# Local attention: the mask instruction scales by the inverse norm and keeps the minimum of negated logits

## The reference, cut to what matters

```
q, k, v = split(shift_token(x) @ wqkv)            # 8 heads of 64
q = l2norm(q) * q_scale;  k = l2norm(k) * k_scale
q, k = rotary_xpos(q, k)
sim  = einsum(q * 8, k)                           # windows of 64: own window and the one before
sim  = where(mask, -finfo.max, sim)               # i < j, or i > j + 64, or j outside
attn = softmax(sim)
x    = x + (attn @ v) @ wo
```

## Time and profile before

| | |
|---|---|
| median of 3 runs | 1843.05 us (1841.29 to 1848.9) |
| profiled execution, span from the first to the last instruction | 1846.8 us |
| busy in it: TensorE, ScalarE, VectorE, GpSimd | 1709.5 us (93%), 1462.7 (79%), 1022.5 (55%), 453.3 (25%) |
| TensorE's granted clock, mean | 0.974 of full speed |
| local attention, first and last exponential | 1112.6 us and 1751.9 us, two layers with a norm and gate between |
| mask instructions, 512 | 117.7 us busy, 285 ns each, and 41.7 us of accumulator reads |
| neg_top products, 128 | 33.9 us busy |
| exponentials, 512 | 245.7 us busy, and 99.3 us of accumulator reads |

### The profile page before, as it was taken

The page is one execution under the profiler, slowest core; times in us unless marked ns, Lnnn a source line. Parts: engine busy times, 40 slices in busy tenths (PEclk is TensorE's granted clock), DMA queues, the critical chain, the costliest instruction groups (busy, mean ns, idle before and its releaser), DMA issues. The chain is left out here.

```text
span 1846.8 us, 67972 instructions
## 1 busy us (share of the span) xinstructions
PE 1709.5 (93%) x27988; PEld 1024.6 (55%) x27988; DVE 1022.5 (55%) x3242; ACT 1462.7 (79%) x2635; POOL 453.3 (25%) x385
## 2 busy tenths in 40 slices
PE   7898799999998999999999978999989879999888
PEld 4675455555554555555555435566663346666633
DVE  5454633334332333443333059999975489999854
ACT  4342599999998999999999948999973379999932
POOL 1113100000000000000000037777730176777400
PEclk9897899999999999999999989999999999999999
DMA  1000211111111111111110031111110001111100
GB/s 60 3 1 26 106 48 50 62 44 62 62 53 45 50 53 53 62 62 49 55 37 31 3 109 27 24 34 34 29 27 11 1 18 33 32 26 31 32 15 34
DMA packets 47439, 73.56 MB, mean 40 GB/s; under 512 B 8400, under 2 KB 38224, under 8 KB 47184
## 3 DMA queue, kind: packets, MB, share of 16 engines
q1 hardware_dynamic: 47184, 69.85, 12.2%
HBM read 21.08 MB, written 2.10 MB: 13 GB/s over the span
## 5 line engine op out<-in xcount | busy, mean ns | idle before, releaser
L689 ACT ACTIVATE x_probs<-x_pss 128x1024 f32<-128x1024 f32 x832 | 806.6, 1021 | 54.3 <-PE x_pss L610 39.6
L624 PE MATMUL x_acc<-x_probs,x_v 128*32 128x256 f32 x6656 | 438.6, 381 | 0.0
L610 PE MATMUL x_pss<-x_qx,x_kx 32*128 32x256 bf16 x9984 | 350.0, 271 | 12.9 <-issue 5.8
L610 PEld LDWEIGHTS x_pss<-x_qx,x_kx 32*128 32x128 bf16 x9984 | 222.2, 93 | 199.9 <-ACT x_probs L689 180.5
L624 PEld LDWEIGHTS x_acc<-x_probs,x_v 128*32 128x32 f32 x6656 | 206.9, 110 | 93.5 <-issue 9.5
L1291 ACT ACTIVATE l_prob<-l_sim,l_neg_top,l_inv_norm 128x128 f32<-128x128 f32 x512 | 245.7, 487 | 4.4 <-DVE l_neg_top L1185 4.4
L736 DVE COPY x_vnext<-x_psp 128x128 f32<-128x128 f32 (+1 forms) x199 | 59.3, 298 | 316.7 <-PE x_psp L588 312.2
L917 POOL TENSOR_TENSOR l_turned_half<-l_raw,l_tabB 128x512 f32<-128x512 f32 x128 | 182.0, 1443 | 60.1 <-ACT l_raw L1250 59.8
L665 POOL COPY x_zq<-zT 128x256 f32 (+1 forms) x15 | 6.0, 402 | 763.1 <-PE x_psp L595 693.5
L927 POOL TENSOR_TENSOR l_direct<-l_direct,l_turned_half 128x1024 f32<-128x1024 f32 x64 | 155.6, 2432 | 0.0
L1177 DVE CUSTOM_DVE_ANT_0 l_sim<-l_pss,w_window 128x128 f32<-128x128 f32 x512 | 117.7, 285 | 3.6 <-issue 2.2
(11 more groups left out here) (185 smaller groups left out, 2642.8 us busy)
## 6 DMA issues: line engine op xcount, KB each, us to landing
x_kx<-x_kp SPq DMA_DIRECT2D x96, 208.0 KB, 2.4
x_cT<-in_context SPq DMA_DIRECT2D x16, 832.0 KB, 4.8
x_qx<-x_qp SPq DMA_DIRECT2D x48, 192.0 KB, 3.2
l_vmid<-l_vt SPq DMA_DIRECT2D x64, 128.0 KB, 2.3
xT<-in_x SPq DMA_DIRECT2D x8, 256.0 KB, 4.4
shifted<-zT SPq DMA_DIRECT2D x32, 64.0 KB, 2.0
hs<-zT SPq DMA_DIRECT2D x32, 64.0 KB, 2.0
out_x<-xT SPq DMA_DIRECT2D x8, 256.0 KB, 2.0
```

The costliest lines, as they stand in the source:

```text
L610: ins = pe.matmul(pss[bank(k, 2 * p + r // 2)][:, r % 2, e, :], kx[par][rows, g, j * P:(j + 1) * P], qx[par][rows, g, a * S:(a + 1) * S], ...
L624: ins = pe.matmul(acc[32 * r:32 * r + 32, 0:S], v[:, j, g, r, :], probs[SLOT[p]][r // 2][:, r % 2, e, :], start=(u == 0), stop=(u == UNITS ...
L689: act.activation(probs[SLOT[p]][y][:, :, :, :], pss[bank(k, 2 * p + y)][:, :, :, :], ACT.Sigmoid, scale=HD ** -0.5).then_inc(weighed, 1)
```

## The change

The sign of the logits is turned in the tables: the cosine and sine of the queries are built with -8 in place of 8, so PSUM holds negated logits. The mask instruction computes (negated logits + window) * inverse norm, with the window 0 inside and +3.0e38 outside, and keeps the minimum of the row, which is the bias that the exponential wants. The separate product and its semaphore go. The exponential becomes exp(-1 * neg_sim + neg_top). The waits move with them: the mask of a block's first group waits for `newton` ahead of its instructions; the inverse norm's buffer is free once the masks, not the exponentials, of two batches before are done.

```diff
-                    at_least(dve, exped, 4 * n - 4)
+                    at_least(dve, masked, 4 * n - 4)
                     dve.scalar_tensor_tensor(inv_norm[r % 2][:, :, :], tmp_b[:, :, :], 1.5, root[:, :, :], ALU.add, ALU.mult).then_inc(newton, 1)
...
                     dve.wait_ge(scored, 2 * n + b + 1)
+                    if h == 0:
+                        dve.wait_ge(newton, 4 * n + 4)
                     at_least(dve, exped, c - 3)
+                    at_least(dve, masked, c)
                     dve.memset(beat[:, :], 0.0)
                     for head in range(HALF * h, HALF * h + HALF):
-                        ins = dve.tensor_tensor_reduce(out=sim[b][:, head, :], in0=pss[head % 2][:, head // 2, :],
-                                                       in1=w["window"][:, b, :], scale=1.0, scalar=NEG, op0=ALU.add,
-                                                       op1=ALU.max, accum_out=top[b][:, head:head + 1])
+                        ins = dve.tensor_tensor_reduce(out=neg_sim[b][:, head, :], in0=pss[head % 2][:, head // 2, :],
+                                                       in1=w["window"][:, b, :], scale=inv_norm[r % 2][:, b, head:head + 1],
+                                                       scalar=FAR, op0=ALU.add, op1=ALU.min,
+                                                       accum_out=neg_top[b][:, head:head + 1])
                     ins.then_inc(masked, 1)
-                    dve.wait_ge(masked, c + 1)
-                    if h == 0:
-                        dve.wait_ge(newton, 4 * n + 4)
-                    at = slice(HALF * h, HALF * h + HALF)
-                    dve.scalar_tensor_tensor(neg_top[b][:, at], top[b][:, at], -1.0, inv_norm[r % 2][:, b, at],
-                                             ALU.mult, ALU.mult).then_inc(negated, 1)
...
-                    act.wait_ge(negated, c + 1)
+                    act.wait_ge(masked, c + 1)
                     at_least(act, turned, c - 3)
                     for head in range(HALF * h, HALF * h + HALF):
-                        ins = act.activation(prob[b][:, head, :], sim[b][:, head, :], ACT.Exp,
-                                             bias=neg_top[b][:, head:head + 1], scale=inv_norm[r % 2][:, b, head:head + 1],
+                        ins = act.activation(prob[b][:, head, :], neg_sim[b][:, head, :], ACT.Exp,
+                                             bias=neg_top[b][:, head:head + 1], scale=-1.0,
                                              accum_out=total[b][:, head:head + 1])
...
-    by_scale = lambda v: np.stack([v * xpos * 8.0, v / xpos], 1)
+    by_scale = lambda v: np.stack([v * xpos * -8.0, v / xpos], 1)
...
-    window = np.full((P, 2, P), NEG, np.float32)
+    window = np.full((P, 2, P), FAR, np.float32)
```

More of the change, by code:

```diff
@@ L35 @@
 HC = (HID + P - 1) // P
-NEG = -3.0e38
+FAR = 3.0e38
 def shift_in(sp, shifted, zT, landed, n):
@@ L820, in local_attention @@
         vmid = [sb(f"vmid{u}", [P, INNER]) for u in range(2)]
-        sim = [sb(f"sim{b}", [P, FH, P]) for b in range(2)]
+        neg_sim = [sb(f"neg_sim{b}", [P, FH, P]) for b in range(2)]
         prob = [sb(f"prob{b}", [P, FH, P]) for b in range(2)]
         probT = [sb(f"probT{b}", [P, FH, P]) for b in range(2)]
-        top, neg_top = [sb(f"top{b}", [P, FH]) for b in range(2)], [sb(f"neg_top{b}", [P, FH]) for b in range(2)]
+        neg_top = [sb(f"neg_top{b}", [P, FH]) for b in range(2)]
         total, inv_total = [sb(f"total{b}", [P, FH]) for b in range(2)], [sb(f"inv_total{b}", [P, FH]) for b in range(2)]
@@ L841, in local_attention @@
         mid_landed = [sem(f"mid_landed{u}") for u in range(2)]
-        scored, masked, negated, exped = sem("scored"), sem("masked"), sem("negated"), sem("exped")
+        scored, masked, exped = sem("scored"), sem("masked"), sem("exped")
         inverted, normed, turned, copied = sem("inverted"), sem("normed"), sem("turned"), sem("copied")
```

## The result

The changed kernel takes 1824.78 us (median of 4 runs, 1823.1 to 1827.18), the kernel before beside it on the same chip 1842.17 (1840.1 to 1848.9). The ratio is 0.9895, with a 95% interval of 0.9869 to 0.9922. Six further runs of it gave 1825.03 (1822.62 to 1826.42).

The account below looks back on a forecast made before the run. The bound was a ring of VectorE with GpSimd against ScalarE with TensorE, arriving within 0.1 us. Turns 6.2, collisions 10 and layer ends 2.4 sum to 18.6 us off 1843: 1824 forecast, range 1810 to 1849.

Parts of the forecast that it names:

- the ends of layers: At each layer's end nothing hides ScalarE; 16 shorter exponentials on its chain count 1.2 us, together 2.4 us.
- The collisions (10 us): Second normalisation on VectorE waits for GpSimd's turn_halves, 1.06 us in ten turns; all ten waits go, about 10 us.
- T: Time mark in each turn: the end of VectorE's first long normalisation, norm(x,0,1).
- the 0.10 us that I had: TensorE's flip_k, forecast to end 0.10 us earlier against T, 0.34 less 0.24, so at T-0.12.
- Rivals 1, 2 and 5: Second-normalisation waits on GpSimd stay, 1834 (0.20); come every turn, 1851 (0.14); nothing measurable changes, 1843 (0.05).
- The 0.24 us a turn: VectorE and GpSimd's part of a turn shortens by 0.24 us; 13 turns in two layers give 6.2 us.
- the product of group (1,1) no longer stands between L927 and L936 on GpSimd: Between inverse norm and T, removing neg_top's product closes a GpSimd gap of 0.15 us, of which 0.14 counted.
- There I had 0.1: VectorE from second normalisation to next inverse norm: two groups, forecast to save about 0.1 us a turn.
- The pointer: Mask instruction on VectorE pays 0.057 us for its inv_norm pointer, 0.23 a group, 0.91 us a turn.
- Rival 3: The pointer makes the mask compete with GpSimd, some 0.75 us a group, 84 us in all: 1908, chance 0.05.
- Rival 4: The pointer is nearly free in a mask instruction and the collisions go too, 12 us more: 1812, chance 0.11.
- 0.91 against 1.4 us a turn: VectorE engine time: mask pointers cost 0.91 us a turn, dropping neg_top's product saves 1.4, net 0.5.

Follow-up runs that it names:

- experiment 1: Kernel before, with the exponential's scale pointer replaced by the constant 1.0 and neg_top still made by a same-shaped instruction: 1827.32 us, ratio 0.9901.
- experiment 2: Changed kernel, with the exponential's scale read through a pointer to a column of -1 instead of the constant: 1848.3 us, ratio 1.0018.
- experiment 4: Kernel before, with the second normalisation, norm(x,1,0), moved ahead of add(x-1) in VectorE's turn: 1846.42 us, ratio 0.9992.
- experiment 3: Changed kernel, with the mask's scale the constant 1.0 instead of the pointer to the inverse norm: 1824.79 us, ratio 0.988.
- experiment 5: Kernel before, with the mask's constant 1.0 read through a pointer to a column of ones and neg_top kept: 1944.16 us, ratio 1.0534.
- experiment 7: Changed kernel with four beat tiles and fewer waits ahead of the masks: 1830.77 us; with satisfied waits for constants in their place: 1827.59 us.
- experiment 6: Changed kernel plus one 128x4 VectorE instruction behind mask(x,1,0): two-input scalar_tensor_tensor 1927.02 us, copy 1918.97 us, reciprocal 1828.87 us.

## Why the prediction was right, and where not

**The total.** 1824 was forecast and 1824.8 measured. Of the sum of 18.6 us, 16.2 were for turns and 2.4 for the ends of layers. Twelve turns of each layer gave 7.3 + 8.6 = 15.9 by the profile (ten collisions and about 0.27 us a turn, less 1.2 for the new long normalisation in layer one) and the tails 2.55; the fillings and the stages outside moved by +1.9 and -5.2 for themselves.

**The collisions (10 us).** Right, in size and cause. They went because the exponentials are shorter: alone that gives nearly the whole gain (experiment 1), and without it they are back (experiment 2). flip_k gained more against T than the 0.10 us that I had, 0.12 to 0.25 (it ends at T-0.13 to T-0.27 now). Rivals 1, 2 and 5 fall with this. That removing a collision is worth its 1.06 us holds here because nothing else was delayed by it, as it was in experiment 4.

**The 0.24 us a turn.** The size was near and the place wrong, so the agreement of this term is luck. The step that failed is "the product of group (1,1) no longer stands between L927 and L936 on GpSimd", 0.14 of the 0.24. Without any product the gap is still 1231.96-(1229.45+2.37) = 0.14: GpSimd takes it between two instructions of its own of which one needs the other, and inverse norm to T stayed at 5.37. What shortened is the other stretch, from place_keys to the inverse norm: 9.29 instead of 9.39 to 9.83, mean 9.50. There I had 0.1; it is 0.21. Experiment 1 has 9.41, so nearly half of this too is ScalarE's. In the kernel before TensorE's score matmuls waited 14 times, 6.4 us in all, for ScalarE's copies of the queries (l_qT), in experiment 1 not once; that these waits are the 0.14 us by which some turns exceed 9.39 is likely and not shown.

**The pointer.** 0.057 was forecast, from another kind of instruction, and 0.06 measured from start to start (0.27 for 0.21). Rival 3 is out in the form I gave it: the 512 masks last 339 to 354 ns, with not one outlier. The Trainium skill (SBUF — State Buffer, "Who interferes with whom") counts inputs in SBUF and lets an instruction with one go, except in its 2-port modes, an exception that the prediction left out. Here window is that one, and the pointer does not count as a second, by the 512 masks beside a GpSimd that is busy for 127.7 of 167 us. Rival 4 was half right: its price hardly matters in the changed kernel (experiment 3), but because 0.48 us of slack lie in front of GpSimd, not because it is small, and its 12 us are not there to be had.

**What the prediction missed.** It priced the pointer and the product one by one, 0.91 against 1.4 us a turn, as if they could be added. They can't: the pointer with the product kept costs 94 to 98 us, 3.2 us a turn (experiment 5), since it pushes the product behind the start of a GpSimd instruction. So a price like rival 3's was in the kernel, by another mechanism: it lies in what stands behind the masks. The change escapes it by taking away the two-input instruction in the same edit; with the exponential left as it was, both together gain nothing (experiment 2). It missed as well that two waits moved ahead of the masks cost 0.14 us behind the inverse norm, which the turn hides (experiment 7).

**The exponential.** 400 ns and 44 us were forecast, 395 and 47.5 measured. The Trainium skill (ScalarE: Activation LUTs, "What ACT_TABLE_LOAD costs") gives about 93 ns for a pointer operand of this kind; the rows agree, with 487-395 = 92. My 0.085 came from starts rounded to 0.01.

**What stays open.** Why VectorE paused for 0.46 us ahead of one memset at 1162.28, which led to the long normalisation at 1166.44. The pause is in both profiles of the changed kernel, and in those of experiments 2 and 3, at the same turn of layer one; with constants in place of the waits (experiment 7) it is in layer two; no kernel without the two waits has it, nor has experiment 6, which keeps them, ahead of a layer's last turn. So the waits are needed for it, and something that small changes of the program move. Open is also how the variation in the stages before layer one comes about.

## What to carry to other kernels

Where VectorE and GpSimd both read operands in SBUF, ask of each small VectorE instruction not what it costs but when it starts: here the same 128x4 instruction lasted 0.17 us ahead of the start of a GpSimd instruction and 2.2 behind it. Before adding 0.06 us to anything, look at how far the next two-input instruction or copy stands from GpSimd's next start; a reciprocal there lasted 0.17 us, and the reductions of `sums` took 1.21 us beside GpSimd as elsewhere. And test the halves of a change apart, each with the other undone: here one half was nearly the whole gain, and the other's two parts cost and saved amounts that only make sense together.

## What the runs showed of the hardware that I had not expected

- A VectorE copy of 128x4 from SBUF to SBUF is held by a running GpSimd instruction for the rest of it (2.23 us long, 0.15 us behind its start), as one with two SBUF inputs is (2.19); a reciprocal of the same shape is not (0.17), nor is a mask instruction that reads PSUM, one SBUF tile and an SBUF pointer (0.35 in 512 instances).
- A VectorE instruction that waits when GpSimd passes from one instruction to the next is let in between: 0.20 us ahead of the boundary it lasted 0.79 us, 0.03 us behind it 1.80.
- A satisfied wait is not free: with two more of them, on a register's value or on a constant alike, the memset followed the inverse norm after 0.29 us in most turns instead of 0.15.
- Fewer instructions were not faster: without those waits VectorE stood still for 2.27 and 2.43 us, with packets of the instruction queue beside both, and the median of 12 runs was 5.7 us above that of 6 runs of the kernel with the waits (1821.13 to 1848.4 against 1822.62 to 1826.42).
